# Attention head of a transformer block: q and k in two halves of the partitions, staging buffers at the end of the work space, and a later wait for the staged rows

## The reference

```python
def _L0_attn_ref(x, w_attn, w_proj, embk, embv):       # x is (8, 512, 128), 16 heads of 8
    q, k, v = jnp.split(x @ w_attn, 3, axis=2)         # each to (B, H, T, d)
    rel = jnp.tril(idx[:, None] - idx[None, :])
    rk, rv = embk[rel], embv[rel]                      # 128 relative positions
    att = einsum('bhtd,bhsd->bhts', q, k) * scale + einsum('bhtd,tsd->bhts', q, rk)
    att = softmax(where(causal, att, -inf))
    y = einsum('bhts,bhsd->bhtd', att, v) + einsum('bhts,tsd->bhtd', att, rv)
    return y.transpose(0, 2, 1, 3).reshape(B, T, C) @ w_proj
x = x + _L0_attn_ref(_layernorm(x), ...)
x = x + _L0_ffn_ref(_layernorm(x), ...)                # 8 experts, top 2, and 2 shared ones
```

## Time and profile before

| | us |
|---|---|
| median of 3 timed runs | 943.62 |
| lowest and highest of them | 940.10, 944.53 |
| the profiled execution | 949.27 |
| its span in the profile | 947.7 |
| PE busy | 717.4 (76%) |
| DVE busy | 605.8 (64%) |
| ACT busy | 529.3 (56%) |
| POOL busy | 262.4 (28%) |

### The profile page before, as it was taken

One profiled execution on the slowest core, in us unless ns is written; L12 is line 12 of the kernel. 1 busy time (PEld: TensorE's weight loads), 2 busy tenths in 40 slices (PEclk: granted clock), 3 DMA queues, 4 the chain that ended last, 5 costly groups with the idle time before them and its releaser, 6 DMA issues. The chain is left out here.

```text
span 947.7 us, 27167 instructions
## 1 busy us (share of the span) xinstructions
PE 717.4 (76%) x10380; PEld 513.2 (54%) x10380; DVE 605.8 (64%) x1930; ACT 529.3 (56%) x1106; POOL 262.4 (28%) x252
## 2 busy tenths in 40 slices
PE   3552277787777887787887787888319999799997
PEld 2331155566565665665666655666216666466664
DVE  4822267685767685766686767777245767647776
ACT  3442278676768575767586777776064334243342
POOL 9411044343334442334452335443000000000000
PEclk9766599999999899999899999999659999999999
DMA  9598758767658776668767659642320000000000
GB/s 303 187 259 255 200 178 267 207 174 206 179 186 263 206 191 177 169 188 241 229 189 193 184 177 262 202 146 74 88 91 1 12 12 12 12 1 11 11 11 11
DMA packets 115675, 141.37 MB, mean 149 GB/s; under 512 B 7088, under 2 KB 81248, under 8 KB 115552
## 3 DMA queue, kind: packets, MB, share of 16 engines
q1 hardware_dynamic: 115552, 139.72, 50.4%
HBM read 82.81 MB, written 56.89 MB: 147 GB/s over the span
## 5 line engine op out<-in xcount | busy, mean ns | idle before, releaser
L801 ACT ACTIVATE work<-ps,nmin 128x128 f32<-128x128 f32 (+3 forms) x512 | 250.0, 537 | 135.2 <-DVE nmin L862 101.3
L862 DVE CUSTOM_DVE_ANT_0 ps<-ps,near 128x128 f32<-128x128 f32 (+3 forms) x512 | 242.5, 509 | 91.7 <-PE ps L683 63.5
L695 PE MATMUL ps<-ident,work 128*128 128x128 f32 x1280 | 213.6, 286 | 80.5 <-ACT work L790 75.4
L695 PEld LDWEIGHTS ps<-ident,work 128*128 128x128 f32 x1280 | 142.3, 144 | 118.3 <-ACT work L790 103.0
L847 DVE COPY work<-ps 128x512 f32<-128x512 f32 (+1 forms) x192 | 123.4, 643 | 86.7 <-PE ps L695 78.5
L683 PE MATMUL ps<-qkb 128*128 128x128 bf16 (+3 forms) x512 | 129.3, 305 | 35.2 <-ACT work L801 32.0
L652 POOL TENSOR_SCALAR_AFFINE_SELECT work<-work 128x512 f32<-128x512 f32 x96 | 61.1, 636 | 330.2 <-ACT work L790 314.0
L656 POOL TENSOR_TENSOR work<-work 128x512 f32<-128x512 f32 x96 | 124.5, 1297 | 8.0
L1219 ACT ACTIVATE silu<-h_ps 128x512 f32<-128x512 f32 x80 | 47.8, 597 | 134.3 <-PE h_ps L1182 134.1
L1194 PEld LDWEIGHTS y_ps<-w_sb,hT 128*128 128x128 f32 x640 | 82.6, 191 | 35.4 <-issue 30.6
L712 PE MATMUL ps<-work,vb 128*9 128x128 f32 x2560 | 96.2, 278 | 6.7 <-ACT relS L779 6.0
(11 more groups left out here) (104 smaller groups left out, 690.8 us busy)
## 6 DMA issues: line engine op xcount, KB each, us to landing
near<-w_slots SPq DMA_DIRECT2D x96, 512.0 KB, 4.6
w_slots<-relS SPq DMA_DIRECT2D x128, 256.0 KB, 4.3
qk_rows<-work SPq DMA_DIRECT2D x48, 256.0 KB, 4.4
qkb<-qk_rows SPq DMA_DIRECT2D x32, 384.0 KB, 5.7
near<-w_slots SPq DMA_DIRECT2D x32, 256.0 KB, 5.0
w_slots<-near SPq DMA_DIRECT2D x8, 512.0 KB, 5.8
v_dram<-work SPq DMA_DIRECT2D x4, 576.0 KB, 6.1
vb<-v_dram SPq DMA_DIRECT2D x4, 576.0 KB, 5.8
```

Of the source, the lines that this page charges most:

```text
L695: ins = nc.tensor.transpose(tp_ps[:, m % 2, n * P:(n + 1) * P], prob[:, m % PROBS, n * P:(n + 1) * P], ident[:, :])
L801: ins = nc.scalar.activation(prob[:, m % PROBS, h * wide:(h + 1) * wide], qk_ps[:, m % 3, h * wide:(h + 1) * wide], ACT.Exp, bias=nmin[:, ...
L862: nc.vector.tensor_tensor_reduce(out=scores, in0=scores, in1=near[:, q % NEAR, a, 4 * P - wide:4 * P, r], scale=1.0, scalar=3e38, op0=ALU. ...
```

## The change

- **q and k in two halves.** `qkb` becomes `qb` (32 heads x 512) and `kb` (16 x 512). Even heads of a quad lie in partitions 0 to 47, odd heads in 64 to 111. In `qb` each head has its own columns, with zeros in the other half; in `kb` an even and an odd head share theirs. The tables te, ek, k127 and rowsel are filled for both halves. A quad's load is now 4 transfers of 48 partitions x 2 heads x 1 KB (q and k of side 0, q and k of side 1), 96 KB each. POOL clears `qb`, and DVE clears `kb` at the start. This frees 16 KB a partition.
- **Staging at the end.** `parts` moves behind all other staging buffers, to the words at STAGE and behind, over which y, rvn and the small buffers lie later, and vg lies over the second half of pcT. WORK grows.
- **The wait moves.** `wait_rows` stands no longer before ACT's first exponential, but before the first av copy on ACT (it writes y), before quad 8 on POOL (it writes the second half of pcT) and before `load_v(1)` on SP.
- **Values of group 0** are written by DVE straight into `vb`; their store and `load_v(0)` go.
- **SP's order** is new: three masks, rows(0), four quads' loads, rows(1), five masks, four quads' loads, rows(2), the first three puts and gets, rows(3).

```diff
@@ SBUF layout and staging @@
-WORK = PROBS * T + 8 * T + 4 * P + 2 * P * NH + 2 * GB * T + NH * D + 2 * C + GB * C + GB * P + 2 * GB * C
+BASE = [0, P // 2]
+STAGE = PROBS * T + 8 * T + 4 * P + 2 * P * NH
+WORK = STAGE + 6 * GB * NI * P
...
-    xs_v, sq_v, xnT_v, parts_v, k32, rest_v, vg_v = carve(
-        t["work"][:, :], TILES * C, GT * C, 2 * GT * P, 6 * GT * P, GT * P, 2 * GT * P, 2 * GT * H * VD)
+    xs_v, sq_v, xnT_v, k32, rest_v, _, vg_v = carve(
+        t["work"][:, 0:STAGE], TILES * C, GT * C, 2 * GT * P, GT * P, 2 * GT * P, GT * P, 2 * GT * H * VD)
+    parts_v = t["work"][:, STAGE:WORK]
...
-    NOUT = 2 * NPART + 1
+    NOUT = [2 * NPART + (g > 0) for g in range(G)]
...
+        if g == 0:
+            return
         sp.wait_ge(vg_done, g + 1)
...
+    def values(g):
+
+        return vg[:, g % 2, :, :, :] if g else t["vb"][:, 0, :, :].rearrange("p n (h d) -> p n h d", d=VD)
...
-        nc.gpsimd.memset(t["qkb"][:, :, :, :].bitcast(F32), 0.0)
+        nc.gpsimd.memset(t["qb"][:, :, :].bitcast(F32), 0.0)
...
+        nc.vector.memset(t["kb"][:, :, :].bitcast(F32), 0.0).then_inc(kb_done, 1)
@@ load_qk @@
-                    src = qk_rows[:, :, h:h + 4, g * GB + b, :, :].rearrange("r d h k t -> (r d) h (k t)")
-                    dst = qkb[0:KR, 4 * u:4 * u + 4, :, :].rearrange("p h k t -> p h (k t)")
-                    sp.dma_start(dst, src).then_inc(qkb_in[u], 16)
+                    for side, base in enumerate(BASE):
+                        src = qk_rows[:, :, h + side:h + 4:2, g * GB + b, :, :]
+                        sp.dma_start(qb[base:base + KR, 4 * u + side:4 * u + 4:2, :],
+                                     src[:, :, :, 0, :].rearrange("r d h t -> (r d) h t")).then_inc(qkb_in[u], 16)
+                        sp.dma_start(kb[base:base + KR, 2 * u:2 * u + 2, :],
+                                     src[:, :, :, 1, :].rearrange("r d h t -> (r d) h t")).then_inc(qkb_in[u], 16)
@@ SP @@
                 first["loads"](sp)
+                first["masks"](sp, range(3))
                 first["rows"](sp, 0)
-                first["rows"](sp, 1)
...
                 for u in range(4):
                     load_qk(0, u)
-                load_v(0)
+                first["rows"](sp, 1)
+                first["masks"](sp, range(3, WSLOTS))
+                for u in range(4, QUADS):
+                    load_qk(0, u)
                 first["rows"](sp, 2)
...
                 get_near(REL_AT.count(0) - 1)
-                for u in range(4, QUADS):
-                    load_qk(0, u)
                 first["rows"](sp, 3)
-                first["wait_rows"](sp)
+                sp.wait_ge(*first["masks_out"](WSLOTS))
@@ load_v(1), quad 8 on POOL, the first av copy and the first exponential on ACT @@
+                            if q == 0:
+                                first["wait_rows"](sp)
                             load_v(q // QUADS // NI + 1)
...
+                    if q == QUADS:
+                        first["wait_rows"](pool)
                     near_probs(q)
...
+                    if n == 0:
+                        first["wait_rows"](act)
                     act.wait_ge(av_done, 4 * n + 4)
...
-                first["wait_rows"](act)
                 for m in range(SLOTS):
```

More of the change, by code:

```diff
@@ L188, in qkv_part @@
     vg = vg_v.rearrange("p (g n h d) -> p g n h d", g=2, n=GT, d=VD)
-    ek = ek[0:KR, :]
-    ekr = ekr_v[0:KR, :].rearrange("p (k n) -> p k n", k=2)
-    ekp = ekp_v[0:KR, :].bitcast(BF16).rearrange("p (k n) -> p k n", k=3)
+    ekr = ekr_v.rearrange("p (k n) -> p k n", k=2)
+    ekp = ekp_v.bitcast(BF16).rearrange("p (k n) -> p k n", k=3)
     stat = sb("stat", [P, 5, TILES], F32)
     rstd = sb("rstd", [P, TILES], F32)
-    k127 = sb("k127", [KR, 1], F32)
+    k127 = sb("k127", [P, 1], F32)
     k127h = sb("k127h", [P, 1], F32)
@@ L197, in qkv_part @@
     eps = sb("eps", [P, 1], F32)
-    rowsel = sb("rowsel", [KR, 3], F32)
+    rowsel = sb("rowsel", [P, 3], F32)
     xT_ps = ps[:, 2:8:5, :]
@@ L233, in qkv_part @@
     mask_out = sem("mask_out")
+    kb_done = sem("kb_done")
     x_tiles = x.rearrange("b (i p) c -> p (b i) c", p=P)
-    NOUT = 2 * NPART + 1
+    NOUT = [2 * NPART + (g > 0) for g in range(G)]
     def sync_loads(sp):
@@ L254, in sync_loads, with masks @@
         sp.wait_ge(mask_done, 3)
-        for n in range(WSLOTS):
+    def masks(sp, lot):
+        for n in lot:
             sp.dma_start(w_slots[n].rearrange("p a c h -> p a (c h)"),
@@ L266, in sync_rows @@
                              ).then_inc(out_done[g % 2], 16)
+        if g == 0:
+            return
         sp.wait_ge(vg_done, g + 1)
         sp.dma_start(v_dram[:, g * GT:(g + 1) * GT, :],
-                     vg[:, g % 2, :, :, :].rearrange("p n h d -> p n (h d)")).then_inc(out_done[g % 2], 16)
+                     values(g).rearrange("p n h d -> p n (h d)")).then_inc(out_done[g % 2], 16)
+    def values(g):
+        return vg[:, g % 2, :, :, :] if g else t["vb"][:, 0, :, :].rearrange("p n (h d) -> p n h d", d=VD)
     def wait_rows(engine):
         for n in range(2):
-            engine.wait_ge(out_done[n], 16 * NOUT * G // 2)
+            engine.wait_ge(out_done[n], 16 * sum(NOUT[n::2]))
     def pool_program(pool):
@@ L280, in pool_program @@
                                 base=0, pattern=[[-1, P]], channel_multiplier=1).then_inc(id_done, 1)
+        nc.gpsimd.memset(values(0)[:, :, :, D:VD], 1.0)
         nc.gpsimd.memset(vg[:, :, :, :, D:VD], 1.0).then_inc(ones_done, 1)
@@ L345, in split @@
             h = g % 2
-            wait(act, out_done[h], 16 * NOUT * (g // 2))
+            wait(act, out_done[h], 16 * sum(NOUT[h:g:2]))
             act.wait_ge(q_ready, 2 * g + 2)
@@ L400, in split @@
             dve.wait_ge(v_ready, g + 1)
-            wait(dve, out_done[h], 16 * NOUT * (g // 2))
+            wait(dve, out_done[h], 16 * sum(NOUT[h:g:2]))
             if g == 0:
@@ L405, in split @@
                 ins = nc.vector.tensor_tensor(
-                    vg[:, h, 4 * n:4 * n + 4, :, 0:D],
+                    values(g)[:, 4 * n:4 * n + 4, :, 0:D],
                     v_ps[:, n, :].rearrange("p (n h d) -> p n h d", h=H, d=D),
@@ L446, in vector_program @@
                 tables()
-    return {"loads": sync_loads, "rows": sync_rows, "wait_rows": wait_rows, "first_rows": (out_done[0], 16 * NOUT),
-            "masks_out": (mask_out, 16 * WSLOTS), "cleared": (mask_done, 4), "tables": (tab, 10), "wp_in": wp_in,
+    return {"loads": sync_loads, "rows": sync_rows, "wait_rows": wait_rows, "first_rows": (out_done[0], 16 * NOUT[0]),
+            "masks": masks, "masks_out": lambda n: (mask_out, 16 * n), "cleared": ((mask_done, 4), (kb_done, 1)), "tables": (tab, 9), "wp_in": wp_in,
             "pool": pool_program, "tensor": tensor_group, "ready": tensor_ready, "scalar": scalar_program,
@@ L459, in attention_part @@
         sem = lambda name: ctx.enter_context(nc.semaphore(name))
-        ident, te, tv, wp, qkb, near = t["ident"], t["te"], t["tv"], t["wp"], t["qkb"], t["near"]
+        ident, te, tv, wp, qb, kb, near = t["ident"], t["te"], t["tv"], t["wp"], t["qb"], t["kb"], t["near"]
         vb = sb("vb", [P, 2, GB * NI, H * VD], F32)
@@ L469, in attention_part @@
                          w_slots)
+        assert 2 * GB * T + NH * D + 2 * C + GB * C + GB * P + 2 * GB * C <= WORK - STAGE
         prob, pT, ptmp, pcT, y, rvn, ysum, yn, ynT, x1 = carve(
@@ L596, in _ @@
                 first["loads"](sp)
+                first["masks"](sp, range(3))
                 first["rows"](sp, 0)
-                first["rows"](sp, 1)
-                sp.wait_ge(*first["cleared"])
+                for signal in first["cleared"]:
+                    sp.wait_ge(*signal)
                 sp.wait_ge(*first["first_rows"])
@@ L602, in _ @@
                     load_qk(0, u)
-                load_v(0)
+                first["rows"](sp, 1)
+                first["masks"](sp, range(3, WSLOTS))
+                for u in range(4, QUADS):
+                    load_qk(0, u)
                 first["rows"](sp, 2)
-                sp.wait_ge(*first["masks_out"])
+                sp.wait_ge(*first["masks_out"](3))
                 for q in range(NQ):
@@ L705, in av @@
                     if e % NI == 0 and u == 0:
-                        pe.wait_ge(v_in[g % 2], 16 * (g // 2 + 1))
+                        wait(pe, v_in[g % 2], 16 * ((g + 1) // 2))
                     bank = misc("av", q // 4)
@@ L1296, in block_kernel @@
              "wp": sb("wp", [P, C], F32),
-             "qkb": sb("qkb", [P, NH, 2, T], BF16),
+             "qb": sb("qb", [P, NH, T], BF16),
+             "kb": sb("kb", [P, NH // 2, T], BF16),
              "near": sb("near", [P, NEAR, 2, 4 * P, 2], F32)}
@@ L1312 @@
     turn = (np.arange(NREL)[None, :] - np.arange(P)[:, None]) % NREL
+    twice = lambda rows: np.tile(np.pad(rows, ((0, P // 2 - KR), (0, 0))), (2, 1))
```

(4 more changed lines are left out.)

25 lines of the change are left out of this document (12 added, 13 removed).

## The result

| | before | after |
|---|---|---|
| median, 8 runs each | 943.35 us | 933.38 us |
| lowest and highest | 938.64, 946.12 | 927.63, 937.06 |
| profiled execution | 949.27 us | 933.78 us |
| its span | 947.7 us | 932.2 us |

The ratio is 0.9881, with a 95% interval of 0.9846 to 0.9916: 1.2% faster, 10 us of the median. The forecast was 933.5. The ratios, here and in the experiments, leave out a few executions that fell in a slower state, over 1.5% above the fastest of their kernel; the medians keep them.

A forecast was written before the change was run, and what follows sets the result against it. The issue of `get_near(3)`, behind the staged rows in SP's ordered queue, was taken as the bound. Summed transfers moved it from 116.98 to 106.8; 10.2 us off the 943.62 median gave 933.4, said as 933.5, range 923 to 944.

The forecast's parts named there:

- get 3: Issue of the fourth quad's `get_near` on SP, said to set the kernel's end: 116.98 to about 106.8, 10.2 us earlier.
- One for one: Everything behind the issue of `get_near(3)` was said to follow its shift in full, 10.2 us.
- The moved waits: `wait_rows` at its new places on ACT, POOL and SP comes after the last row landed: costs nothing.
- get 0: Issue of the first `get_near` on SP, put at 87.8 instead of 81.56.
- the returned wait of 7.5 us: At q = 3, DVE waits for near 3, giving back 7.5 of the first exponential's 18.7 us.
- A lot of loads: Four quads' q and k loads in the head, put at 10.4 us by the rate of one side.
- overlap of the two halves: Rival on the q and k loads: sides don't queue behind each other, 8.2 us more saved, 925; chance 0.20.
- the late masks: Five masks behind rows(1) and v(1) in SP's order: 2.62 MB at 408 GB/s, 6.4 us.
- The floor for small transfers: Rival on the loads: 96 KB transfers cost about 1 us each, a lot 16 us, gain gone, 944; chance 0.14.
- The hidden parts: POOL's halved clear, DVE's 3.4 us clear of kb and the added load issues lie under existing waits: nothing.
- The 33 us of added issues: Three more load issues in each of 24 quads on SP, hidden in its 26.9 us of put waits: 0.
- The signs of being wrong: DVE waiting for near in query tile 3, ACT several us at the first av copy, PE for loads at a group's start.

The follow-up runs named there:

- Kernel 2: Changed kernel with SP's old order (all eight masks, rows(0) and rows(1) ahead of the first loads): ratio 0.9892 to the kernel before.
- kernel 4: Changed kernel with rows(3) in pieces behind the puts of q = 3 to 5 instead of ahead of the fourth put: ratio 0.9802 to the kernel before.
- kernel 1: Changed kernel with ACT's wait for all staged rows put back before its first exponential: 940.61 us, ratio 0.9937 to the kernel before.
- kernel 3: Changed kernel with all eight masks ahead of rows(0): 929.37 us, ratio 0.9837 to the kernel before.
- kernel 7: Changed kernel with all eight masks first and rows(3) in pieces between the puts: 922.86 us, ratio 0.9758 to the kernel before.
- Kernel 8: Changed kernel with masks first and both rows(2) and rows(3) in pieces behind the puts of q = 1 to 6: 921.79 us, ratio 0.9723.
- kernel 5: Kernel before with each quad's load cut into four 96 KB transfers, all to partitions 0 to 47: ratio 0.9982 to the kernel before.
- kernel 6: Changed kernel with a lot's eight transfers of side 0 first, then the eight of side 1: one execution, 941.18 us.
- kernel 9: Changed kernel with a quad's four transfers alternating sides (q side 0, q side 1, k side 0, k side 1): one execution, 944.53 us.

## Why the prediction was right

**What binds.** That get 3, not the first exponential, sets the end: shown from both sides. Kernel 2 has the first exponential 9.3 us earlier than the change and no gain; kernel 4 has it where the change has it and get 3 10.9 us earlier, and gains 7.5.

**"One for one"** was probably too much, and here it did no harm. Against the change, get 3 comes 10.1 us later in the kernel before and 4.6 in kernel 1, for 10 and 5 us of time. Earlier gets give less than they are: 6.05, 10.9 and 16.7 us (kernels 3, 4 and 7) for 4, 7.5 and 12 us, each of these good to some 5 us. The moved waits were put at nothing, and in the change they cost nothing: its first av copy, at 122.85, waits 0.16 us, and for PE. Kernel 8 shows that this is a matter of where the rows stand.

**The two times.** get 0 was put at 87.8 and came at 86.36; get 3 at 106.8 and came at 106.89. The first exponential at 93.1 came at 91.52, and the returned wait of 7.5 us was 8.75.

**The terms of the sum** were less exact than its result. A lot of loads was put at 10.4 us; by an estimate from windows of 2 us its traffic took about 8.5 (41 to 48 and 67 to 73 have 197 and 195 GB/s). The step that was mis-sized is the choice of the one-sided rate for two sides: kernels 5, 6 and 9 show that sides in alternation relieve each other, 154 GB/s for one side, 161 for two apart, 193 by twos, 208 and issue-bound by turns. So the rival "overlap of the two halves" was half true, and it had less to give than its 8.2 us. Against this the late masks went at 377 instead of 408 GB/s, rows(2) at 351 instead of 383 in the middle of its stretch:

```profile
76.00:82.00 6.00, 0.00 (x0) 0.00 (x0) 0.00 (x0) 0.00 (x0) 0.00 (x0) 0.50 1.04 351
```

The masks are 0.5 us more by that, and rows(2) with v 1.0. The staging began 0.9 us later (28.76 against 27.89), but the first lot was issued at 39.45, where the sum had 39.5. Two lots of about 2 us less, and 2 to 3 us more elsewhere, left get 0 1.4 us early; the gets and rows(3) behind it then took 20.5 us instead of 19. Part of the hit at get 3 is thus cancelling, and that the time fell on 933.4 is luck to within these 2 us.

The Trainium skill's page "SBUF — State Buffer", section "Can I just issue two DMAs to hit both halves?", answers no, with plus 6% for two concurrent transfers. Here the trace differs: with 96 KB transfers of the two sides next to each other in one queue, the rate is 25% above that of such transfers to one side (193 against 154 GB/s), and the DMA engines cease to be the bound when they alternate one by one. For sides apart in the queue the rule holds (161 against 154). The same page of the Trainium skill, in its section "Door 1: The DMA port swizzle", gives each port of the memory a rate in bytes; kernel 5 agrees with that, 154 GB/s with packets of 1 KB as 150 with 2 KB.

**The floor for small transfers**, the rival at 944: out. 96 KB transfers went out every 0.47 us in the changed kernel's first lot (39.45 to 46.45 for 16).

**The hidden parts.** POOL's and DVE's clears, from the timelines of the two engines:

```profile
7.79 6.92 POOL L301 MEMSET qb<- 128x8192 f32 x1
```

```profile
1.77 3.47 DVE L448 MEMSET kb<- 128x4096 f32 x1 [0.83 <-issue]
7.66 0.15 DVE L450 TENSOR_SCALAR nk127h<-k127h 128x1 f32<-128x1 f32 x1 [2.42 <-DMA vb<-in_e_v]
```

kb took 3.47 us (3.4 in the sum) and DVE still waited 2.42 us for its data. The 33 us of added issues were hidden too, but with less to spare than was said. SP's waits between 188 and 240, the stretch that answers to the earlier trace rows:

```profile
SPq L590 <- ACT relS L801: 20.0, 9, 2.8
SPq L598 <- DMA w_slots<-relS: 5.3, 9, 1.9
```

SP's waits for a put to land are 5.3 us in 9 times, 0.6 each, where 3.0 were; a quad's 1.4 us of issues and what they hold up have taken most of that cover. SP now waits instead for the rel copy, 20.0 us in 9 times, so there is slack left, in another place. In kernel 5, with the same number of issues and the old order, the waits for a landing are 13.5 us between 200 and 250. The signs of being wrong did not come: between 125 and 735 the changed kernel has no wait of PE for a load of q and k, and DVE's waits for `near` there are 11.5 us, where the kernel before has 21.7.

**Not settled.** The two profiled executions differ by 15.5 us and the medians by 10. The first x1 tile is stored 12.1 us earlier (196.43 and 184.29), and the difference then wanders between 9.8 and 19.0 us over the tiles. The moved transfers don't explain this, and kernels with the same head differ as much: kernel 5 stores the first tile 0.9 us before the kernel before, and the ninth 12.2 us. The largest step, from 9.8 to 19.0 us, lies between the sixth and the ninth tile, and the granted clock differs there. About these tiles, in the kernel before, then in the changed one:

```profile
350.00:480.00 130.00, 103.02 (x2170) 78.14 (x2170) 87.95 (x308) 88.77 (x194) 48.70 (x51) 0.96 0.69 200
```

```profile
338.00:460.00 122.00, 97.34 (x2149) 74.94 (x2148) 86.53 (x304) 87.54 (x194) 47.67 (x49) 1.00 0.69 207
```

For nearly the same matmuls PE is busy 103.0 us at a clock of 0.96, and 97.3 at 1.00. So a part of the 15.5 us is probably the clock's in one execution. Whether the change has a hand in that no run here shows; I take it for the scatter of single executions, since the medians of 8 runs differ by 10 us, as get 3 does.

## What to carry to other kernels

When an engine has stood long before a wait, look for the next thing that the work behind the wait will need, and read how close that one is today: here 1 us of slack at the fourth quad decided what 20 us at the first were worth. On a queue that one engine issues in order, a lot that nobody needs soon belongs into the issuer's own waits between links of the chain that binds, not ahead of them; filling an idle gap with it brings nothing if other transfers are pushed from free time into the busy stretch to make the room. Here rows(3) in pieces between the puts, and the masks left where they were free, brought the ratio to the kernel before from 0.988 to 0.976. And when a bulk lot is pushed back, look at who waits for its landing: with rows(2) pushed back too, the wait that had just been moved out of the way was met again (kernel 8).
